# Split fp32r products for the projections, values out of the key projection, logits with experts as columns, and the first transfers on two queues

## What is computed

```python
q, k, v = x @ wq.T + bq, x @ wk.T + bk, x @ wv.T + bv    # 16 query heads, 4 key and value heads of 16
q, k = rope(q), rope(k)             # the angle depends on the head, not on the position
att = softmax(where(tril, q @ k.T / 4, -inf));  y = (att @ v) @ cp.T + cp_b
x = layernorm(x + y)
scores = sigmoid(x @ gate.T) + gate_b            # 16 experts
weights, indices = top_k(scores, 4);  weights /= weights.sum()
x = layernorm(x + shared_expert(x) + sum(weights * experts[indices](x)))
```

## Time and profile before

| | |
|---|---|
| time, median of 3 runs | 551.11 us (550.45 to 555.86) |
| span of the profiled execution | 548.3 us |
| PE busy | 525.8 us (96%) |
| DVE busy | 435.9 us (79%) |
| ACT busy | 372.3 us (68%) |
| POOL busy | 290.6 us (53%) |

### The profile page before, as it was taken

The page is one execution under the profiler, slowest core; times in us unless marked ns, Lnnn a source line. Parts: engine busy times, 40 slices in busy tenths (PEclk is TensorE's granted clock), DMA queues, the critical chain, the costliest instruction groups (busy, mean ns, idle before and its releaser), DMA issues.

```text
span 548.3 us, 12215 instructions
## 1 busy us (share of the span) xinstructions
PE 525.8 (96%) x3796; PEld 359.4 (66%) x3796; DVE 435.9 (79%) x1126; ACT 372.3 (68%) x841; POOL 290.6 (53%) x336
## 2 busy tenths in 40 slices
PE   8999999999999899989999898899999999999885
PEld 4656444444554454534433387799999999999874
DVE  2388989899889899999992177987878788787685
ACT  2444777787888688968879566366766667667534
POOL 5121232555412777267978856477644454545292
PEclk9999999999999999999999999999999999999999
DMA  5934174400523811321042352378544443341495
GB/s 150 179 66 65 31 191 145 82 8 21 91 62 88 207 58 46 82 81 51 32 128 82 104 178 66 112 227 262 159 139 128 130 118 111 111 133 46 160 414 194
DMA packets 53710, 64.96 MB, mean 118 GB/s; under 512 B 8091, under 2 KB 47406, under 8 KB 53648
## 3 DMA queue, kind: packets, MB, share of 16 engines
q1 hardware_dynamic: 45968, 46.45, 31.4%
q0 software_dynamic: 7056, 17.60, 9.2%
q10 hardware_dynamic: 624, 0.13, 0.1%
HBM read 32.49 MB, written 25.62 MB: 106 GB/s over the span
## 4 chain that ended last, share of the span: by engine, by line
PE 75%; DVE 10%; POOL 6%; issue 3%; ACT 2%; DMA 2%; SPq 1%; POOLq 0%; DVEq 0%; ACTq 0%
PE psH L1705 13%; PE psS L1506 12%; PE psO L1491 11%; PE psT L1476 10%; PE psS L1568 4%; PE psX L1673 3%; PE psG L1716 3%; PE psS L1511 2%; PE psS L1592 2%; POOL xs_scratch L766 2%; PE psY L1733 2%; PE psY L1730 2%; PE psY L1729 2%; PE psY L1732 2%; PE psY L1731 2%
## 5 line engine op out<-in xcount | busy, mean ns | idle before, releaser
L885 ACT ACTIVATE prob<-psT 128x512 f32<-128x512 f32 (+3 forms) x384 | 167.3, 495 | 51.6 <-PE psT L1476 49.0
L1161 DVE TENSOR_REDUCE MX<-psS 128x1 f32<-128x512 f32 (+3 forms) x344 | 182.6, 595 | 9.1 <-PE psS L1511 3.9
L1506 PE MATMUL psS<-KS,QS 96*128 96x512 bf16 (+3 forms) x384 | 109.9, 328 | 4.4 <-DVE MX L1161 2.5
L839 POOL DMA_INDIRECT y_scratch<-ys,dst x79 | 76.9, 973 | 65.7 <-ACT ys L1040 50.8
L1476 PE MATMUL psT<-QS,KS 98*128 98x512 bf16 (+3 forms) x384 | 107.0, 328 | 0.9 <-ACT prob L885 0.4
L795 POOL TENSOR_SCALAR_AFFINE_SELECT prob<-prob 128x512 f32<-128x512 f32 x64 | 42.4, 665 | 91.8 <-ACT prob L885 91.6
L1491 PE MATMUL psO<-prob,V 128*32 128x512 f32 (+3 forms) x768 | 81.3, 498 | 1.2 <-POOL prob L795 1.2
L1705 PE MATMUL psH<-wU,xh 128*128 (+1 forms) x380 | 80.8, 334 | 0.5 <-DVE z L1313 0.4
L766 POOL DMA_INDIRECT xs_scratch<-x1row,slotu x64 | 65.4, 1022 | 26.9 <-issue 16.2
L1476 PEld LDWEIGHTS psT<-QS,KS 98*128 98x128 bf16 x384 | 33.7, 97 | 52.9 <-ACT prob L885 34.6
L1506 PEld LDWEIGHTS psS<-KS,QS 96*128 96x128 bf16 x384 | 37.1, 98 | 45.4 <-DVE MX L1161 22.5
(11 more groups left out here) (260 smaller groups left out, 1003.0 us busy)
## 6 DMA issues: line engine op xcount, KB each, us to landing
xs<-xs_scratch SPq DMA_DIRECT2D x80, 134.0 KB
y<-y_scratch SPq DMA_DIRECT2D x16, 512.0 KB, 10.2
QS<-qp SPq DMA_DIRECT2D x48, 128.0 KB, 4.5
wU_raw<-in_L_ffn_w_routed_dram SPq DMA_DIRECT2D x32, 176.0 KB, 2.9
xs_scratch<-padrow SPq DMA_DIRECT2D x1, 2144.0 KB
xs_scratch<-padrow SPq DMA_DIRECT2D x16, 134.0 KB
x1row<-in_L_attn_x_dram SPq DMA_DIRECT2D x4, 512.0 KB, 5.8
out_dram<-x1row SPq DMA_DIRECT2D x7, 256.0 KB, 2.6
```

What stands on the lines that cost most here:

```text
L839: nc.gpsimd.indirect_dma_start(y4_dram, bass.IndirectOffsetOnAxis(ap=dst[:, n % NSEL, t:t + 1], axis=0), ys[:, n % NYS, t, :], None, bound ...
L885: nc.scalar.activation(prob[:, step % NPROB, h, 0:HALF - c0], ps[:, 0:HALF - c0], ACT.Exp).then_inc(s_Tfree, 1)
L1161: found = nc.vector.tensor_reduce(out=MX[:, c0 // HALF, heads[0]:heads[-1] + 1, i - TH * q], in_=src, op=ALU.max, axis=AX_X)
L1506: last = mm(ps[:, e * dist:e * dist + cols], QS[0:ROWS, QAT[(k // 2) % NSLOT], g % 2 * G + h, (i - TH * q) * P:(i - TH * q + 1) * P], KS[b ...
```

## The change

It does six things.

1. Input and weights of the projections are split: ACT writes a high part in fp32r, DVE the rest in fp32r (`xTl`, `wqTl`, `wkvTl`). A projection is then six fp32r products of 512 columns: high by high, high by low, low by high, for two blocks of 128 rows of the contraction. The items `xT` and `wS` (the weights) now use the banks that DVE frees.
2. The value weights stand beside the keys' weights (`wkvT`, 128 columns), so a key projection gives the values in rows 64 to 127. ACT copies them to `VT`, and the item `v` is eight transposes.
3. A gate has the weights stationary: 8 fp32 products with 16 output rows and 128 columns, four tiles in four column groups; a new item `turn` transposes the result back, and DVE copies both.
4. The first queries are sent from POOL, the first keys from SP; their third parts are made on DVE (`FIRST_SPLITS`). The small first loads are put in another order: keys' weights first.
5. The low parts lie at the end of the experts' weights `wA`, so the loads of its last eight experts wait on SP for all splits.
6. `ORDER` is another table.

```diff
@@ first_items @@
+    if b == 0:
+        return ([("wS", 1)] + [("xT", b, k, 0) for k in range(KC)] +
+                [("wS", 2), ("wS", 0), ("proj", b, 0, 0), ("wT", 4), ("proj", b, 1, 0)])
...
@@ tensor: proj, v, gate, turn @@
-    for k in range(KC):
-        last = mm(ps[0:rows, 0:HALF], wT[:, k, :],
-                  xT[:, k, half * HALF:(half + 1) * HALF], start=(k == 0), stop=(k == KC - 1))
+    parts = [(w, x, k) for k in range(KC) for w, x in ((high, xT), (high, xTl), (low, xT))]
+    for w, x, k in parts:
+        last = mm(ps[:, 0:HALF], w[:, k, :], x[:, k, c], start=((w, x, k) == parts[0]), stop=((w, x, k) == parts[-1]))
...
     for i in range(TT):
-        for k in range(KC):
-            last = mm(ps[:, i * KVW:(i + 1) * KVW], xT[:, k, i * P:(i + 1) * P], wvT[:, k, :],
-                      start=(k == 0), stop=(k == KC - 1))
+        last = nc.tensor.transpose(ps[:, i * KVW:(i + 1) * KVW], VT[KVW:P, i * P:(i + 1) * P], ident[KVW:P, KVW:P])
...
-    for i in range(TH):
-        for k in range(KC):
-            last = mm(ps[:, i * NE:(i + 1) * NE], x1T[:, k, i * P:(i + 1) * P], gwT[:, k, :],
+    for k in range(KC):
+        for i in range(TH):
+            last = mm(ps[32 * i:32 * i + NE, 0:P], gwT[:, k, :], x1T[:, k, i * P:(i + 1) * P],
                       start=(k == 0), stop=(k == KC - 1))
+elif kind == "turn":
+    pe.wait_ge(s_Sfree, S_NO[("gate",) + item[1:]])
+    nc.tensor.transpose(ps[:, 0:P], lgT, ident[:, :]).then_inc(s_S, 1)
...
@@ vector @@
+if kind == "xT":
+    dve.wait_ge(s_high, HIGH_NO[item])
+    nc.vector.tensor_tensor(xTl[:, k, c], ps[:, :], xT[:, k, c].bitcast(F32), ALU.subtract).then_inc(s_Sfree, 1)
...
@@ scalar: proj @@
+    if m == 0:
+        nc.scalar.copy(VT[KVW:P, half * HALF:(half + 1) * HALF], psS[KVW:P, (S_NO[item] - 1) % 4, 0:HALF]).then_inc(s_vt, 1)
...
@@ gpsimd @@
+if item == ("qload", 0):
+    for part in range(3):
+        queries(pool, 0, part)
...
@@ sync: freed @@
+if u[0] == "wA" and 2 * u[2] * C * 4 > 2 * NX * C * 4 - 4 * (KC * T + KC * C + KC * 2 * KVW):
+    sp.wait_ge(s_part3, LOWS)
...
@@ vector: smax @@
+    if k:
+        dve.wait_ge(s_T, T_NO[("mrow", k - 1)])
@@ ORDER @@
-aaaaaaaadadpaaldppdlpdaaaapalaaaaapaapamalpppaxxaaaxxaaxaalxxxaaxxvamaxxavxxxaaaxavaxaxpaxmaxaxaaxxaaxvxaaaxxaexpavmaaxx
+aaaaaappaaddppplplaaaaaaaadaadapaalmpapadpaxaxlxaaxxaaxaxxapvmxaxalxxavaxxxaaaxdxaaxaxpaaxvvmxxaxaxaxeaxaxaxavaxxaxpxavv
```

More of the change, by code:

```diff
@@ L159, in weight_units @@
     after[("wB", 0, 3)] = projected
+    for c in (3, 4, 5):
+        after[("wA", 3 * c, min(3 * c + 3, NX))] = projected[0:-2]
     after[("wU", 1)] = [("kload", B - 1, half) for half in range(NHALF)]
@@ L233 @@
 PROJ_NO, CP_NO, LN_NO = count("proj"), count("cp"), count("ln")
+HIGH_NO = count("xT", "wS")
 SEL_NO = {item: n + 1 for n, item in enumerate(
@@ L505, in attention_moe, with low_part, queries_in, queries @@
         st2 = x1L[:, 0, 0, 0:6 * NT].rearrange("p (i a) -> p i a", i=NT)
+        def low_part(item):
+            n = PROJ_NO[("proj",) + item]
+            return (s_first3, n) if n <= len(FIRST_SPLITS) else (s_part3, n - len(FIRST_SPLITS))
+        LOWS = len(PROJ_NO) - len(FIRST_SPLITS)
+        def queries_in(s):
+            if s == 0:
+                return s_first_q, 16 * len(PAIRS)
+            return s_qload[s % NSLOT], 16 * len(PAIRS) * (s // NSLOT + (s % NSLOT > 0))
+        def queries(engine, s, part):
+            b, q, g = HEADGROUPS[2 * s]
+            m = g // 2
+            if part < 2:
+                engine.wait_ge((s_part1, s_part2)[part], PROJ_NO[("proj", b, 1 + m, q)])
+            else:
+                engine.wait_ge(*low_part((b, 1 + m, q)))
+            for a, pair in enumerate(PAIRS):
+                if pair[0] == part:
+                    engine.dma_start(QS[a * HD:(a + 1) * HD, QAT[s % NSLOT], :, :],
+                                     qp[:, m, part, q * HALF:(q + 1) * HALF]).then_inc(queries_in(s)[0], 16)
+        lgT = hit[:, :, :, :].rearrange("p i k e -> p (i k e)")[:, 0:P]
         def tile_of(b, i):
@@ L627, in run @@
                         keys_part(b, half, part)
-                        if (b, half) == (0, 0):
-                            queries_part(0, part)
                 elif kind == "qload":
@@ L637, in run @@
                         for part in range(3):
-                            queries_part(s, part)
+                            queries(sp, s, part)
                     if s == 0:
@@ L1135, in run @@
                     dve.wait_ge(s_ones[1], 2)
-                if kind == "proj":
+                if kind == "xT":
+                    _, b, k, half = item
+                    if b and (k, half) == (0, 0):
+                        dve.wait_ge(s_S, max(S_NO[("proj", b - 1, m, h)] for m in range(KC + 1) for h in range(NHALF)))
+                    dve.wait_ge(s_high, HIGH_NO[item])
+                    c = slice(half * HALF, (half + 1) * HALF)
+                    nc.vector.tensor_tensor(xTl[:, k, c], ps[:, :], xT[:, k, c].bitcast(F32), ALU.subtract).then_inc(s_Sfree, 1)
+                elif kind == "wS":
+                    dve.wait_ge(s_high, HIGH_NO[item])
+                    c = slice(0, KVW) if item[1] == 1 else slice(KVW, 2 * KVW)
+                    high, low = (wkvT[:, :, c], wkvTl[:, :, c]) if item[1] else (wqT[:, :, :], wqTl[:, :, :])
+                    width = KC * KVW if item[1] else KC * C
+                    nc.vector.tensor_tensor(low, ps[:, 0:width].rearrange("p (k o) -> p k o", k=KC), high.bitcast(F32),
+                                            ALU.subtract).then_inc(s_Sfree, 1)
+                elif kind == "proj":
                     _, b, m, half = item
@@ L1552, in run @@
                                                            cp_n[:, m, k * P:(k + 1) * P], ident[:, :])
-                    last.then_inc(s_T, 1)
+                    last.then_inc(s_S if kind == "wS" else s_T, 1)
                 elif kind == "xT":
```

200 lines of the change are left out of this document (118 added, 82 removed).

## The result

| | before | changed |
|---|---|---|
| time, median of 20 runs each (lowest to highest) | 551.89 us (550.45 to 558.73) | 548.33 us (545.81 to 554.30) |
| ratio to the kernel before, 95% interval | | 0.992 (0.9895 to 0.9945) |
| span of the profiled execution | 548.3 us | 545.6 us |
| PE busy | 525.8 us (96%) | 511.7 us (94%) |
| DVE busy | 435.9 us (79%) | 442.9 us (81%) |

The account below looks back on a forecast made before the run. The attention was taken as limited by PE, then DVE, then POOL. Start -0.8, PE -3.2, gates -0.5 + 0.75, tail +0.5 sum to -3.25: span 545.0, plus 2.8 is 547.8, stated as 547.5 us, range 541.5 to 554.5.

Parts of the forecast that it names:

- Prices: Projections to 180 us: six products 1.35 us (bounds 1.0 to 1.5), eight transposes 0.9, four DVE low parts 0.69 each.
- I let PE's 3.2 us count in full: First scores to 180 us: PE's saving on projections and values, 3.2 us, shortens the time by all of it.
- the weight loads only where SP now waits for the last low part: At about 120 us: loads stand on SP ahead of a maxima row's transfer; cost taken as 0.
- [DVE's 3.5 us] lie in DVE's 14.6 us of room: 28 to 180 us: DVE's added low parts and remainder, 3.5 us, are covered by its 14.6 us of idle time.
- The rival that made DVE the limit: From 28 us on PE's saving becomes idle: +4.0, 555.1 us; decided by DVE idle above 11 us; chance 0.12.
- The start: Before the first scores: transfers set the queries' landing; first maximum at 27.3 us, 0.8 earlier, between 25.2 and 31.
- The clock at the start: First head group: PE may fall to 1.2 GHz, 6.0 us instead of 3.0, nearly covered by DVE's maxima; taken as 0.
- Gates: 180 to 291 us: three gates save 0.5 us of a possible 4.5 on PE, DVE's copies cost 0.75.
- The tail: Second ranking to last select: ranking 2.5 us earlier, POOL's list 3.1 us longer, together +0.5, bounds -2 to +4.
- the slots' delay to use up the slack and no more: Third quarter's ranking in the tail: slots about 3 us later, against 3.3 us of slack before POOL's scatter.
- such a wait as a sign of being wrong: Tail: POOL waiting for slots after the last maximum would make the tail longer by that wait.
- The prediction's own signs of being right: Projection 1.3 to 1.4 us, DVE idle 6 to 10, first maximum 26.5 to 28, last select 3 to 4 earlier.

Follow-up runs that it names:

- Experiment 3: Changed kernel with ACT's first split of an expert's weights placed 19 items later in the order: 545.06 us, ratio 0.9866 to the kernel before.
- Experiments 7 and 8: DVE's remainder of the second batch's six projections made three times over, in the changed kernel (558.80 us, ratio 1.0109) and in the kernel before (559.58 us, 1.0144).
- experiment 2: Changed kernel with 24 products of ones on PE in the wait before the first scores: 551.22 us, ratio 0.9981 to the kernel before.

## Why the prediction was right in sum, step by step

**Prices: near.** A projection takes 1.50 us from its first row to the next instruction (32.49 to 33.99; 1.35 forecast, 1.5 as the upper bound): 0.23 each, and 0.34 for the first product. The eight transposes take 0.64 (83.60 to 84.24; 0.9 forecast). So PE saves about 2.3 us of the 3.2 on these, and 1.0 more on the first gate, which lies in the same stretch. DVE's four low parts are 2.7 us as forecast; the remainder of a projection did not come on top, since either kernel makes seven in the stretch.

**"I let PE's 3.2 us count in full": failed in the kernel as it is.** Up to the first ranking nothing is gained. The forecast looked at the weight loads only where SP now waits for the last low part, at about 120 us; the wait came from the same list 40 us earlier, on ACT, for the first load. Experiment 3 takes it away and finds 3.5 us, for some 3.3 that PE saves there with the gate, so PE's time does count in this order; the stall was missed.

**"[DVE's 3.5 us] lie in DVE's 14.6 us of room": the reason failed.** Experiments 7 and 8 put work there and it counts eight to nine tenths by the stretch. Idle time of DVE in this stage is best read as time behind PE or ACT in a hand-over of four banks. In experiment 3 the new order does carry 1.5 us more of DVE's work in a shorter stretch (idle 9.20 us for 14.25); that it can because PE and DVE have other things to do meanwhile is argued, not shown. The rival that made DVE the limit had named 11 us of idle time to 180 us as its sign, and 12.8 were measured; its price did not follow, since the idle time held the stall.

**The start: right mechanism, size off.** The transfers set it, and the second queue saves nothing; but 0.1 us was gained for 0.8. The input stands among the queries with all of its 1.9 us.

**The clock at the start: right.** It falls, and DVE covers it (experiment 2). Not seen: three later falls, each behind a wait of 1.7 to 2.5 us.

**Gates: prices right.** What the term gives was not measured by itself. PE takes 0.62 + 0.27 us for one, 1.85 before; DVE's copies are 0.29 and 0.21 us, for the 0.22:

```profile
222.70 0.62 PE L1711 MATMUL psS<-x1T,gwT 128*16 128x128 f32 x16
...
224.64 0.27 PE L1717 MATMUL psS<-ident,hit 128*128 128x128 f32 x1
...
223.39 0.29 DVE L1302 COPY hit<-psS 128x128 f32<-128x128 f32 x1 [0.29 <-PE psS L1711]
```

**The tail: mis-sized, and the gain is here.** The forecast had the second ranking 2.5 us earlier for four maxima put behind it, and POOL's list 3.1 us longer from there, +0.5 together. The first half came true by its number (-2.6), though the stretch also holds the collision of DVE and POOL told in the last section, which was not forecast. The second did not: POOL's list before was not closed from the slots on. Two waits of the kernel before stand in it:

```profile
245.46 0.64 POOL L795 TENSOR_SCALAR_AFFINE_SELECT prob<-prob 128x512 f32<-128x512 f32 x1 [0.61 <-ACT prob L885]
...
248.62 0.57 POOL L801 TENSOR_TENSOR rs<-ve,eps_pow 128x1 f32<-128x1 f32 x1 [2.52 <-DVE ve L1200]
```

They add to 3.1 us and are gone in the changed kernel. Its one wait there is for the third slots, 1.74 us; the prediction took the slots' delay to use up the slack and no more, and named such a wait as a sign of being wrong:

```profile
289.11 1.00 POOL L819 DMA_INDIRECT xs_scratch<-x1row,slotu  x1 [1.74 <-DVE slotu L1344]
...
307.19 1.81 POOL L852 TENSOR_SCALAR_AFFINE_SELECT prob<-prob 128x512 f32<-128x512 f32 x3
```

From the second slots to the end of the last select, before and after (columns as in the stages):

```profile
243.80:311.42 67.62, 64.78 (x461) 26.82 (x461) 47.64 (x127) 54.38 (x127) 55.35 (x64) 1.00 0.21 72
```

```profile
241.07:309.00 67.93, 62.74 (x460) 26.63 (x452) 51.42 (x137) 54.27 (x122) 57.77 (x64) 0.97 0.22 78
```

POOL is busy 2.4 us longer and idle 2.1 us less, which is the 0.3 us.

So of the sum -0.8 - 3.2 + 0.25 + 0.5 the profiles give -0.1, 0, and -2.3 for the last two together. 547.5 was hit by two errors of opposite sign. The prediction's own signs of being right show it: none of the four came in its range. The projection takes 1.50 us (1.3 to 1.4), DVE is idle 12.8 us up to 180 us (6 to 10), the first maximum starts at 28.01 (26.5 to 28, missed by a hair), and the last select ends 2.4 us earlier (3 to 4).

## What to carry to other kernels

Cut two profiles at the same work, not at the same time, before asking which part gained: here the totals agreed and the parts did not. When an edit makes the engine that limits a stage faster, look in the new order for whatever that engine will now reach too early, a load above all; one weight split placed 19 items too early took 3 of some 7 us of gain. And count idle time as room only where the order puts other work into it; test it by adding a lump there.
